# A two-layer relational graph network with two expert stages: counting spread over the edge tiles, its products three tiles later, four banks for sums, clearing in halves

## The chip, the core and the metric

The kernel runs on one core of one Trainium2 chip. The metric is the device time of one execution in microseconds (us), the median over runs. TensorE multiplies matrices, VectorE and ScalarE work on tiles, GpSimd issues the indirect row gathers, and SyncE's queue (SP) issues the other DMAs. Each engine works through its own list in order; semaphores tie the lists together.

## What is computed

The input is 2500 nodes of 256 features and 40000 edges sorted by destination, each with one of 8 relation types. Four residual blocks follow one another: a relational graph network of two layers, a mixture of experts, a three-layer graph convolution, a second mixture. The change lies in the first block, and a little of it in the third:

```python
def _rgcn_layer(x, W, self_w, b, src, dst, edge_type, num_nodes):
    xW = jnp.einsum('ni,rio->rno', x, W)
    msg = xW[edge_type, src]
    agg = jax.ops.segment_sum(msg, dst, num_segments=num_nodes)
    return agg + x @ self_w + b
...
x = x + _L0_gnn_ref(_layernorm(x, axis=-1), L0_gnn_W1, L0_gnn_self_w1, L0_gnn_b1, L0_gnn_W2, L0_gnn_self_w2, L0_gnn_b2, edge_index, edge_type_8)
x = x + _L0_ffn_ref(_layernorm(x, axis=-1)[None], L0_ffn_Wg, L0_ffn_bg, L0_ffn_W1, L0_ffn_b1, L0_ffn_W2, L0_ffn_b2)[0]
x = x + _L1_gnn_ref(_layernorm(x, axis=-1), edge_index, L1_gnn_W1, L1_gnn_b1, L1_gnn_W2, L1_gnn_b2, L1_gnn_W3, L1_gnn_b3, L1_gnn_Wp, L1_gnn_bp)
x = x + _L1_ffn_ref(_layernorm(x, axis=-1)[None], L1_ffn_Wr, L1_ffn_br, L1_ffn_ln_g, L1_ffn_ln_b, L1_ffn_W1, L1_ffn_b1, L1_ffn_W2, L1_ffn_b2)[0]
```

## The kernel before

A relational layer (`relational_layer`) walks over 313 edge tiles of 128 edges, one per step `t`. Every engine runs through the same steps in its own list, and the code of a step says what that engine issues there.

- GpSimd gathers the 128 source rows of a tile (line 1120). ScalarE makes a one-hot matrix of each edge's relation and place among 16 destinations (lines 1208 and 1211).
- TensorE multiplies rows by one-hots (`aggregate`, line 1374; each of its two products is two instructions) into one of the three PSUM banks `psS`. It may write a bank again when VectorE has added its last content: tile `t` waits for the addition of tile `t - 3`.
- VectorE adds the bank to `sums` at a place that depends on the data (`add`, lines 1267 to 1278). The place is read into a register by `value_load`, a register load in VectorE's own list, ahead of the addition.
- When a tile of 128 nodes is complete (`closed(b)`, every 16 steps), VectorE carries its rim over (`merge`) and TensorE multiplies its sums by the weights, 18 products of two instructions each (`multiply`, line 1402), spread over the steps up to `left_at(b)`. VectorE then takes the result (`take_out`, or `row_variance` and a step later `row_norm`), and SP clears the buffer with zeros by one DMA (`clear`, line 1142). There are three such buffers.

Between these lies work for later blocks:

- Counting. The third block needs how often each source occurs for each of 80 buckets of 32 destinations; layer 0 does 44 buckets, layer 1 36, one per 7 steps (`SPACING`). For a bucket VectorE makes one matrix for the sources (line 1328) and six for the pairs (`count_hots`, line 1319), in the bucket's steps 0, 2 and 4: the first of these steps has the source matrix and two pair matrices, the others two pair matrices each. Each of the three steps begins with a `value_load` of the bucket's first edge tile (line 1357). TensorE multiplies two pair matrices (line 1420) one step after each.
- Splitting of expert weights into two halves: a piece of 256 KB is loaded, ScalarE makes the high half, VectorE the low one (line 1335), SP stores both. Each layer has 48 pieces, one per 6 steps; the other 32 are split in the third block's layers (`node_layer`).

In the trace, lines 1278 (the addition), 1319, 1328 (counting) and 1374, 1402, 1420 (TensorE) are the marks to follow.

Of the kernel before, what the change touches and what calls it, by code (L numbers as in the profile page):

```python
# [71 lines left out]
LAYER_UNITS = ([*range(24, 32), *range(0, 4)], [*range(4, 8), *range(16, 24)])  # L72
# [14 lines left out]
ZEROS = SUMW // 9  # L87
STRIPS_FIRST = 11
SPACING = 7
PIECESTEP = 6  # L90
# [19 lines left out]

def left_at(b):

    return closed(b + 1) + 2 if b + 1 < TILES else closed(b) + 6
# [26 lines left out]
class Program:  # L140
# [891 lines left out]
    def relational_layer(self, layer):  # L1032
# [19 lines left out]
        psS, psO, psM, psC = [self.ps[b] for b in (0, 1, 7)], [self.ps[b] for b in (2, 6)], self.ps[3], self.ps[4:6]  # L1052
# [3 lines left out]
        steps = left_at(TILES - 1) + 7  # L1056
# [6 lines left out]
        def products_at(t):  # L1063

            b = next((b for b in range(TILES) if closed(b) + 2 <= t < left_at(b)), None)
            if b is None:
                return None, range(0)
            width, k = left_at(b) - closed(b) - 2, t - closed(b) - 2
            return b, range(PRODUCTS * k // width, PRODUCTS * (k + 1) // width)
# [10 lines left out]
        def strip_at(t):  # L1080

            i = counted_at(t, SPACING + 1)
            return buckets[i] // PER if i is not None and buckets[i] % PER == PER - 1 else None

        def piece_at(t, after):

            n, late = divmod(t - after, PIECESTEP)
            return n if late == 0 and 0 <= n < pieces else None
# [4 lines left out]
        def misc_at(t):  # L1093

            then = [("self", tile_at(closed, t))]
            if not first:
                then += [("turned", tile_at(left_at, t - 3)), ("gate", tile_at(left_at, t - 4))]
            return [(what, b) for what, b in (*then, ("degree", strip_at(t))) if b is not None]
# [4 lines left out]
        with self.stage_block() as (block, sem):  # L1103
            hot_ready, squared, summed, added, merged, out_full, out_taken, h_done, h_stored = sem(
                "hot_ready", "squared", "summed", "added", "merged", "out_full", "out_taken", "h_done", "h_stored")
            misc_full, misc_out, places_ready, src_hot, pair_hot, count_full, bank_out = sem(
# [17 lines left out]
            def _(sp):  # L1124
# [13 lines left out]
                def clear(b):  # L1138
                    sp.wait_ge(out_full, b + 1)
                    to = self.sums[:, b % SUMS * SUMW:(b % SUMS + 1) * SUMW].rearrange("p (a c) -> p a c", c=ZEROS)  # L1140
                    of = self.zero.rearrange("p (a c) -> p a c", a=1).broadcast_to([P, SUMW // ZEROS, ZEROS])
                    sp.dma_start(to, of).then_inc(cleared[b % SUMS], 16)
# [24 lines left out]
                for t in range(steps):  # L1167
                    n = piece_at(t, PIECESTEP // 2 + 2)
                    if n is not None:
                        store_piece(n)  # L1170
                    n = piece_at(t, PIECESTEP + 2)
                    if n is not None and n + 2 < pieces:
                        load_piece(n + 2)
                    b = tile_at(left_at, t)
                    if b is not None:
                        clear(b)
                        if first:
                            store_h(b)
                    b = tile_at(left_at, t - 1)
                    if b is not None and not first:  # L1180
                        store_rows(b)
                    b = strip_at(t)
                    if b is not None:
                        store_strip(b)
# [3 lines left out]
                for s in range(SUMS):  # L1188
                    sp.wait_ge(cleared[s], 16 * len(range(s, TILES, SUMS)))
# [10 lines left out]
            def _(act):  # L1200
# [45 lines left out]
                for t in range(steps):  # L1246
                    if t % GROUP == 0 and t // GROUP + HOTROWS - 1 < BATCHES:
                        onehots(t // GROUP + HOTROWS - 1)
                    b = tile_at(left_at, t)
                    if b is not None:  # L1250
                        relu(b) if first else row_root(b)
                    i = counted_at(t, SPACING - 1)
                    if i is not None:
                        take_counts(i)
                    for what, b in misc_at(t):
                        take(what, b)
                    n = piece_at(t, PIECESTEP // 2)
                    if n is not None:
                        high_piece(n)

            @block.vector
            def _(dve):
# [3 lines left out]
                def add(t):  # L1266
                    at = dve.value_load(self.at[0:1, t:t + 1], min_val=0, max_val=(SUMS - 1) * SUMW + P - 1)
                    to = self.sums[:, bass.ds(at, SUMW)].rearrange("p (s w) -> p s w", w=KEYROW)[:, :, 0:WIN]
                    dve.wait_ge(summed, t + 1)
                    if t:  # L1270
                        dve.wait_ge(added, t)
                    b = tile_at(closed, t - 1)
                    if b is not None and b + 1 < TILES:
                        dve.wait_ge(merged, b + 1)
                    b = tile_at(opened, t)
                    if b is not None and b >= SUMS:
                        dve.wait_ge(cleared[b % SUMS], 16 * (b // SUMS))
                    v.tensor_tensor(to, to, psS[t % len(psS)][:, 0:KD * P].rearrange("p (s w) -> p s w", w=WIN), ALU.add).then_inc(added, 1)  # L1278
# [6 lines left out]
                def take_out(b):  # L1285
                    dve.wait_ge(out_full, b + 1)
                    if b >= 2:
                        dve.wait_ge(h_done, b - 1)
                    v.tensor_tensor(self.hn[b % 2][:, :], psO[b % 2][:, 0:D], self.bias[:, :], ALU.add).then_inc(out_taken, 1)

                def row_variance(b):
                    x, mv = self.x_tile(b), self.mv[:, 2 * b:2 * b + 2]
                    dve.wait_ge(out_full, b + 1)
                    if b == 0:
                        dve.wait_ge(kept, 16)
                    v.tensor_tensor(x, x, psO[b % 2][:, 0:D], ALU.add).then_inc(out_taken, 1)
# [25 lines left out]
                def count_hots_from(i, at, j):  # L1322
                    k = buckets[i]
                    if j == 0:
                        if i >= 2:
                            dve.wait_ge(count_full, (i - 1) * WINDOW)
                        low = self.src_low[:, bass.ds(at, WINDOW)].rearrange("p (s c) -> p s c", c=1).broadcast_to([P, WINDOW, P])
                        v.tensor_tensor(src_hots[i % 2].rearrange("p (s c) -> p s c", s=WINDOW), places_low, low, ALU.is_equal).then_inc(src_hot, 1)
                    for n in range(j, j + 2):
                        count_hots(i, at, n)  # L1330
# [11 lines left out]
                for t in range(steps):  # L1342
# [8 lines left out]
                    b = tile_at(left_at, t - 1)  # L1351
                    if b is not None and not first:
                        row_norm(b)
                    for j in range(0, WINDOW, 2):
                        i = counted_at(t, j)
                        if i is not None:
                            at = dve.value_load(self.window[0:1, buckets[i]:buckets[i] + 1], min_val=0, max_val=ETILES - WINDOW)
                            count_hots_from(i, at, j)
                    n = piece_at(t, PIECESTEP // 2 + 1)
# [4 lines left out]
            def _(pe):  # L1364
# [22 lines left out]
                def multiply(b, which):  # L1387
                    to = psO[b % 2][:, 0:D]
                    for n in which:
                        r, k = divmod(n, KD)  # L1390
                        if n == 0:
# [4 lines left out]
                            if b >= 2:  # L1396
                                pe.wait_ge(out_taken, b - 1)
                        if n == KD * REL:
                            pe.wait_ge(misc_out, nth["self", b] + 1)
                        lhs = sum_of(b, 0, P)[:, k * REL + r, :] if r < REL else self.self_turned[b % 2][:, k * P:(k + 1) * P]  # L1400
                        at = (k * REL + r) * D if r < REL else (KD * REL + k) * D
                        last = t_.matmul(to, lhs, weights[:, at:at + D], start=(n == 0), stop=(n == PRODUCTS - 1))  # L1402
                        if n == PRODUCTS - 1:
                            last.then_inc(out_full, 1)
# [27 lines left out]
                for t in range(steps):  # L1432
# [17 lines left out]
                    for j in range(0, WINDOW, 2):  # L1450
                        i = counted_at(t, j + 1)
# [198 lines left out]
    def node_layer(self, layer):  # L1650
# [15 lines left out]
        with self.stage_block() as (block, sem):  # L1666
# [6 lines left out]
            pieces = max(0, min(TILES, UNITS // 2 * 4 - first_piece))  # L1673
# [680 lines left out]
```

## Time and profile before

| What | Value |
|---|---|
| Time, median of 3 runs | 2360.2 us (2356.88 to 2361.87) |
| The profiled execution | 2363.23 us, its span 2361.5 us |
| Additions of layer 0 (line 1278), first to last | 51.5 to 569.8 us |
| Additions of layer 1, first to last | 596.6 to 1133.7 us |
| Busy share of the span | PE 81%, PEld 69%, DVE 58%, ACT 37%, POOL 38% |

The profile names the engines PE (TensorE), PEld (its weight loads), DVE (VectorE), ACT (ScalarE), POOL (GpSimd). A name with a q, as DVEq, is the engine's own list of instructions that it doesn't count as busy: register loads, semaphore waits. The two relational layers take up almost half of the span, from about 43 to 1150 us.

### The profile page before, as it was taken

What the parts mean: (1) busy time and instruction counts of PE and PEld (TensorE: products, weight loads), DVE (VectorE), ACT (ScalarE), POOL (GpSimd) and SP (SyncE); (2) the same over time, 40 slices, a digit from 0 to 9 for tenths busy, and PEclk for the clock granted to TensorE, in tenths of its full rate; (3) what the DMA queues carried; (4) which work ended last, traced back from release to release, by engine and by line L of the source; (5) the groups of instructions that cost most, each with busy time, mean ns of one, the idle gap of its engine ahead of it and who ended that gap; (6) DMA issues with size and microseconds to landing.
All of it is one profiled execution on the core that took longest, in us unless ns stands there. A gap on an engine that the chain in (4) does not pass through costs nothing. (4 is left out here: it accounts for less than half of the span.)

```text
span 2361.5 us, 41254 instructions
## 1 busy us (share of the span) xinstructions
PE 1917.5 (81%) x11984; PEld 1625.5 (69%) x11984; DVE 1368.9 (58%) x3174; ACT 869.5 (37%) x2015; POOL 893.5 (38%) x859
## 2 busy tenths in 40 slices
PE   3778888887677787788479999949989875899987
PEld 2566666666566666667369999837878765799977
DVE  4666666563566666665455555564645566566654
ACT  4434444341543333443013333334544431333332
POOL 3776565550776555554013433330000000333332
PEclk8999999999898899998769999979999975999998
DMA  6676677663676666666564633245766457324261
GB/s 215 211 238 220 217 222 226 216 219 119 218 240 209 198 209 202 201 220 200 176 263 109 203 64 100 32 142 199 252 206 214 136 205 284 119 42 119 41 201 23
DMA packets 204784, 420.87 MB, mean 178 GB/s; under 512 B 24837, under 2 KB 115953, under 8 KB 200433
## 3 DMA queue, kind: packets, MB, share of 16 engines
q1 hardware_dynamic: 153864, 308.52, 37.3%
q0 software_dynamic: 48096, 106.74, 18.4%
q10 hardware_dynamic: 2568, 2.56, 0.3%
q8 instruction: 117, 1.92, 0.3%
q14 instruction: 139, 1.13, 0.2%
HBM read 256.77 MB, written 113.77 MB: 157 GB/s over the span
## 5 line engine op out<-in xcount | busy, mean ns | idle before, releaser
L2193 PE MATMUL ps<-ring,halves 128*128 x3384 | 581.7, 327 | 17.0 <-SPq L2155 9.3
L2193 PEld LDWEIGHTS ps<-ring,halves 128*128 128x128 f32 x3384 | 485.9, 192 | 61.7 <-issue 18.8
L1278 DVE TENSOR_TENSOR sums<-sums,ps 128x256 f32 x626 | 263.3, 421 | 304.0 <-PE ps L1374 223.2
L1374 PEld LDWEIGHTS ps<-slots,rows 128*128 128x128 f32 x2504 | 393.6, 207 | 61.4 <-ACT slots L1211 26.8
L1374 PE MATMUL ps<-slots,rows 128*128 128x128 f32 x2504 | 406.3, 290 | 25.9 <-DMA rows<-tab_h,gidx_node 14.2
L1120 POOL DMA_INDIRECT rows<-tab_h,gidx_node x313 | 312.6, 999 | 260.0 <-PE ps L1374 117.1
L1402 PE MATMUL ps<-fixed,sums 128*128 128x256 f32 x1280 | 390.8, 400 | 0.2 <-DVE sums L1283 0.2
L1120 POOL DMA_INDIRECT rows<-tab_x,gidx_node x313 | 311.5, 995 | 203.9 <-PE ps L1374 91.8
L1420 PE MATMUL ps<-scratch,fixed 128*128 128x320 f16 x960 | 198.9, 322 | 195.0 <-DVE scratch L1319 189.9
L1420 PEld LDWEIGHTS ps<-scratch,fixed 128*128 128x128 f16 x960 | 65.6, 100 | 329.4 <-DVE scratch L1319 169.9
L2302 ACT ACTIVATE x_all<-ps 128x512 f32<-128x512 f32 x188 | 113.2, 602 | 467.8 <-PE ps L2212 467.8
L1208 ACT ACTIVATE slots<-iota,dst_in_bucket 128x128 f32<-128x128 f32 x626 | 199.2, 390 | 223.0 <-PE ps L1374 213.1
L1859 PE MATMUL ps<-node_rows,blocks 128*128 128x512 f32 (+1 forms) x1200 | 258.7, 367 | 0.1
L1319 DVE TENSOR_SCALAR scratch<-fixed,scratch,count_key 128x640 f16<-128x640 f16 x480 | 198.9, 456 | 72.0 <-issue 71.8
L1859 PEld LDWEIGHTS ps<-node_rows,blocks 128*128 128x128 f32 x1200 | 203.8, 195 | 30.9 <-ACT blocks L1741 0.6
L2260 DVE TENSOR_TENSOR halves<-x_all,halves 128x512 fp32r<-128x512 f32 x188 | 130.2, 692 | 147.5 <-ACT halves L2303 147.5
L1402 PEld LDWEIGHTS ps<-fixed,sums 128*128 128x128 f32 x1280 | 211.6, 201 | 5.2 <-DVE sums L1283 0.6
L1959 POOL IOTA x_all<- 128x20 f32 x2 | 0.3, 148 | 437.7 <-POOLq L214 437.7
L2170 POOL DMA_INDIRECT out<-x_all,place_of_slot x47 | 74.6, 1588 | 205.4 <-ACT x_all L2310 170.7
L2170 POOL DMA_INDIRECT x_sum<-x_all,place_of_slot x47 | 74.4, 1582 | 192.4 <-ACT x_all L2310 149.4
L2270 DVE TENSOR_TENSOR whole<-ps,acc 128x512 f32<-128x512 f32 x188 | 121.2, 686 | 39.7 <-PE ps L2193 35.1
L2162 POOL DMA_INDIRECT x_all<-tab_node,token_of_slot x94 | 93.6, 996 | 122.7 <-POOLq L214 82.3
(245 smaller groups left out, 2144.0 us busy)
## 6 DMA issues: line engine op xcount, KB each, us to landing
ring<-split_weights SPq DMA_DIRECT2D x16, 4096.0 KB, 15.1
split_weights<-fixed SPq DMA_DIRECT2D x192, 256.0 KB
sums<-fixed SPq DMA_DIRECT2D x40, 1152.0 KB, 6.8
slots<-tab_counts SPq DMA_DIRECT2D x40, 640.0 KB, 4.1
fixed<-in_ffn_units SPq DMA_DIRECT2D x96, 256.0 KB, 3.7
split_weights<-weight_pieces SPq DMA_DIRECT2D x64, 256.0 KB, 2.5
tab_counts<-fixed SPq DMA_DIRECT2D x20, 640.0 KB, 5.4
strip<-tab_counts SPq DMA_DIRECT2D x20, 640.0 KB, 4.1
```

What stands on the lines that cost most here:

```text
L1120: nc.gpsimd.indirect_dma_start(rows[:, s * D:(s + 1) * D], None, table, bass.IndirectOffsetOnAxis(ap=gidx[:, t:t + 1], axis=0)).then_inc(g ...
L1208: last = nc.scalar.activation(to[:, j * P:(j + 1) * P], self.iota[:, 0:P], ACT.Square, scale=-1.0, bias=self.rel[:, t:t + 1])
L1278: v.tensor_tensor(to, to, psS[t % len(psS)][:, 0:KD * P].rearrange("p (s w) -> p s w", w=WIN), ALU.add).then_inc(added, 1)
L1319: v.tensor_scalar(pair_hots[j], places, base[:, buckets[i]:buckets[i] + 1], self.key[:, bass.ds(at + j, 1)], ALU.add, ALU.is_equal).then_i ...
L1374: last = t_.matmul(psS[t % len(psS)][:, k * P:(k + 1) * P], rows[:, s * D + k * P:s * D + (k + 1) * P], self.onehots[:, h * P:(h + 1) * P] ...
L1402: last = t_.matmul(to, lhs, weights[:, at:at + D], start=(n == 0), stop=(n == PRODUCTS - 1))
L1420: last = t_.matmul(psC[h][:, 0:half], src_hots[i % 2][:, n * P:(n + 1) * P], pair_hots[n][:, h * half:(h + 1) * half], start=(n == 0), sto ...
L1859: last = nc.tensor.matmul(to, self.blocks[b % 2][:, g * P:(g + 1) * P], self.node_tile(layer, g), start=False, stop=(g == TILES - 1))
L2170: nc.gpsimd.indirect_dma_start(to, bass.IndirectOffsetOnAxis(ap=self.place[:, i:i + 1], axis=0), yout[i % 2], None, compute_op=ALU.add).th ...
L2193: ins = nc.tensor.matmul(to, lhs[left], weights(slot, right, at, n), start=first and (left, right) == (0, 0), stop=last and left == 1)
L2260: nc.vector.tensor_tensor(hT_low[:, b * 512:(b + 1) * 512], hT[:, b * 512:(b + 1) * 512], hT_high[:, b * 512:(b + 1) * 512], ALU.subtract) ...
L2270: last = nc.vector.tensor_tensor(h[:, b * 512:(b + 1) * 512], psH[b][:, :], bias(e, b * 512, 512), ALU.add)
```

## The change

Everything stands in `relational_layer`, apart from constants and one line of `node_layer`.

- Counting: each of a bucket's 7 steps gets one piece: step 0 the source matrix, steps 1 to 6 one pair matrix each. Every one of them is behind a `value_load` of its own. TensorE's products of a bucket come at its steps 5, 7 and 9 (`COUNTED`), each three steps behind the second pair matrix that it reads; ScalarE takes the counts at step 10 (`TAKEN`).
- Banks: `psS` has four banks, so `aggregate` waits for the addition of tile `t - 4`. `psO`, the result of `multiply`, has one bank and waits until VectorE has taken the tile before.
- `multiply` begins three steps after `closed(b)` (`begun`) and is spread over 12 steps, first the products of the buffer's first half, then those of the second. SP clears each half by a DMA of its own, in rows of 384 elements where there were 256.
- ScalarE's and VectorE's row work behind `take_out` and `row_variance` comes one to three steps later than before.
- Weight pieces: one per 7 steps, 44 in each layer; 40 where there were 32 in `node_layer`.

```diff
@@ -69,7 +69,8 @@
-LAYER_UNITS = ([*range(24, 32), *range(0, 4)], [*range(4, 8), *range(16, 24)])
+NODEUNITS = 10
+LAYER_UNITS = ([*range(24, 32), *range(0, 3)], [*range(3, 8), *range(18, 24)])
...
-ZEROS = SUMW // 9
+ZEROS = SUMW // KD // 3
...
-PIECESTEP = 6
+COUNTED = 5
+TAKEN = 10
+HIGHPIECE = 1
+LOWPIECE = 4
...
+def begun(b):
+
+    return closed(b) + 3 if b + 1 < TILES else left_at(b - 1)
+
+
 def left_at(b):
 
-    return closed(b + 1) + 2 if b + 1 < TILES else closed(b) + 6
+    return closed(b) + 15 if b + 1 < TILES else begun(b) + 4
...
-        psS, psO, psM, psC = [self.ps[b] for b in (0, 1, 7)], [self.ps[b] for b in (2, 6)], self.ps[3], self.ps[4:6]
+        psS, psO, psM, psC = [self.ps[b] for b in (0, 1, 6, 7)], self.ps[2], self.ps[3], self.ps[4:6]
...
-                def clear(b):
-                    sp.wait_ge(out_full, b + 1)
...
+                def clear(b, k):
+                    sp.wait_ge(half_used, KD * b + k + 1)
...
+                    b = tile_at(begun, t - 6)
+                    if b is not None:
+                        clear(b, 0)
+                    b = tile_at(left_at, t)
+                    if b is not None:
+                        clear(b, 1)
...
-                def count_hots_from(i, at, j):
-                    k = buckets[i]
-                    if j == 0:
-                        if i >= 2:
-                            dve.wait_ge(count_full, (i - 1) * WINDOW)
...
-                    for n in range(j, j + 2):
-                        count_hots(i, at, n)
...
-                    for j in range(0, WINDOW, 2):
-                        i = counted_at(t, j)
-                        if i is not None:
-                            at = dve.value_load(self.window[0:1, buckets[i]:buckets[i] + 1], min_val=0, max_val=ETILES - WINDOW)
-                            count_hots_from(i, at, j)
-                    n = piece_at(t, PIECESTEP // 2 + 1)
+                    i, late = divmod(t, SPACING)
+                    if i < len(buckets):
+                        at = dve.value_load(self.window[0:1, buckets[i]:buckets[i] + 1], min_val=0, max_val=ETILES - WINDOW)
+                        if late:
+                            count_hots(i, at, late - 1)
+                        else:
+                            source_hots(i, at)
+                    n = piece_at(t, LOWPIECE)
...
-                        r, k = divmod(n, KD)
+                        k, r = divmod(n, REL)
...
-                        i = counted_at(t, j + 1)
+                        i = counted_at(t, j + COUNTED)
...
-            pieces = max(0, min(TILES, UNITS // 2 * 4 - first_piece))
+            pieces = max(0, min(TILES, NODEUNITS * 4 - first_piece))
```

On VectorE in layer 0 this is a bucket's first counting step before, with the next step's addition behind it. `TENSOR_LOAD window` is the counting's register load, `TENSOR_LOAD fixed` that of the addition; an `ISA` row is register arithmetic or a wait.

```order
L1357 TENSOR_LOAD window
L1357 ISA x2
L1328 ISA [waits set0_14]
L1328 TENSOR_TENSOR fixed<-iota,src_in_tile 128x768
L1319 ISA [waits set0_14]
L1319 TENSOR_SCALAR scratch<-fixed,scratch,count_key 128x640
L1319 ISA [waits set0_14]
L1319 TENSOR_SCALAR scratch<-fixed,scratch,count_key 128x640
L1267 TENSOR_LOAD fixed
L1267 ISA x2
L1278 ISA [waits set0_3,set0_2]
L1278 TENSOR_TENSOR sums<-sums,ps 128x16x16
```

And the same place after the change (lines 1341, 1334, 1282 and 1293 are the former 1328, 1319, 1267 and 1278).

```order
L1367 TENSOR_LOAD window
L1367 ISA x2
L1341 ISA [waits set0_15]
L1341 TENSOR_TENSOR fixed<-iota,src_in_tile 128x768
L1282 TENSOR_LOAD fixed
L1282 ISA x2
L1293 ISA [waits set0_3,set0_2]
L1293 TENSOR_TENSOR sums<-sums,ps 128x16x16
L1367 TENSOR_LOAD window
L1367 ISA x2
L1334 ISA [waits set0_15]
L1334 TENSOR_SCALAR scratch<-fixed,scratch,count_key 128x640
```

The two pair matrices have left the step; from here on additions and single pieces of counting alternate, with a register load ahead of each. Over both layers the list has 560 loads of `window` where it had 240, and 626 of `fixed` as before.

On TensorE in layer 0, steps of tiles with the same gathered rows before: the counting products (line 1420) wait for the pair matrices (`set0_13`) made in VectorE's step just before.

```order
L1374 MATMUL ps<-slots,rows 128x128 [waits gathered18,set0_3,set0_0]
L1374 MATMUL ps<-slots,rows 128x128
L1402 MATMUL ps<-fixed,sums 128x256
L1420 MATMUL ps<-scratch,fixed 128x320 [waits set0_13,set0_15,set0_12]
L1420 MATMUL ps<-scratch,fixed 128x320
L1420 MATMUL ps<-scratch,fixed 128x320 [waits set0_13]
L1420 MATMUL ps<-scratch,fixed 128x320
L1374 MATMUL ps<-slots,rows 128x128 [waits gathered19,set0_3,set0_0]
```

After (1387, 1416 and 1436 are the former 1374, 1402 and 1420):

```order
L1387 MATMUL ps<-slots,rows 128x128 [waits gathered22,set0_3,set0_0]
L1387 MATMUL ps<-slots,rows 128x128
L1416 MATMUL ps<-fixed,sums 128x256 [waits set0_6,set0_4]
L1436 MATMUL ps<-scratch,fixed 128x320 [waits set0_14,set0_16,set0_13]
L1436 MATMUL ps<-scratch,fixed 128x320
L1436 MATMUL ps<-scratch,fixed 128x320 [waits set0_14]
L1436 MATMUL ps<-scratch,fixed 128x320
L1387 MATMUL ps<-slots,rows 128x128 [waits gathered23,set0_3,set0_0]
```

A bucket's first products have moved four tiles on, and the products of a node tile begin one tile later than they did.

## Rows read from the trace of the kernel before

**Rows 1.** The page's busy time of each engine: us, share of span, instructions.
```profile
PE 1917.5 (81%) x11984; PEld 1625.5 (69%) x11984; DVE 1368.9 (58%) x3174; ACT 869.5 (37%) x2015; POOL 893.5 (38%) x859
```

**Rows 2.** Windows: layer 0's additions; layer 1 while it counts, and after.
```profile
core 0: us, PE busy (x) PEld busy (x) DVE busy (x) ACT busy (x) POOL busy (x), PEclk, DMA share, GB/s
51.40:569.90 518.50, 417.64 (x2705) 323.61 (x2706) 317.62 (x706) 209.32 (x551) 304.84 (x307) 0.94 0.67 213
596.50:1053.85 457.35, 355.25 (x2234) 279.29 (x2235) 291.66 (x716) 183.25 (x498) 274.72 (x275) 0.90 0.66 209
1053.85:1134.20 80.35, 70.32 (x441) 64.72 (x440) 41.44 (x115) 26.20 (x72) 31.41 (x33) 0.92 0.61 197
```

**Rows 3.** Waits, whole span: who for whom, us in total, times, longest.
```profile
DVE sums L1278 <- PE ps L1374: 223.2, 301, 8.7
...
PE ps L1420 <- DVE scratch L1319: 189.9, 151, 5.5
```

**Rows 4.** VectorE's own list, lines 1267 and 1357: ns minimum/median/maximum, first and last.
```profile
L1267 DVEq TENSOR_LOAD <-fixed x626: 297/308/1483, 42.9 to 1132.9; - x157
L1267 DVEq FUSED_REGOPS  x626: 190/190/206, 43.5 to 1133.3; - x157
...
L1357 DVEq TENSOR_LOAD <-window x240: 297/304/1176, 51.5 to 1050.2; - x120
```

**Rows 5.** Timeline of VectorE, two quiet places: start, length, what, idle before.
```profile
73.32 0.42 DVE L1278 TENSOR_TENSOR sums<-sums,ps 128x256 f32 x1 [0.41 <-PE ps L1374]
74.14 0.42 DVE L1278 TENSOR_TENSOR sums<-sums,ps 128x256 f32 x1 [0.40 <-PE ps L1374]
74.89 0.96 DVE L1328 TENSOR_TENSOR fixed<-iota,src_in_tile 128x768 f16<-128x768 f32 x1 [0.33 <-issue]
75.77 0.80 DVE L1319 TENSOR_SCALAR scratch<-fixed,scratch,count_key 128x640 f16<-128x640 f16 x2
76.48 0.41 DVE L1278 TENSOR_TENSOR sums<-sums,ps 128x256 f32 x1
...
317.30 0.42 DVE L1278 TENSOR_TENSOR sums<-sums,ps 128x256 f32 x1 [0.53 <-PE ps L1374]
318.07 0.80 DVE L1319 TENSOR_SCALAR scratch<-fixed,scratch,count_key 128x640 f16<-128x640 f16 x2 [0.35 <-issue]
319.04 0.42 DVE L1278 TENSOR_TENSOR sums<-sums,ps 128x256 f32 x1 [0.17 <-issue]
```

**Rows 6.** Timeline of VectorE while a buffer is being cleared.
```profile
306.16 0.96 DVE L1319 TENSOR_SCALAR scratch<-fixed,scratch,count_key 128x640 f16<-128x640 f16 x2 [0.71 <-issue]
307.82 0.42 DVE L1278 TENSOR_TENSOR sums<-sums,ps 128x256 f32 x1 [0.69 <-issue]
309.67 0.42 DVE L1278 TENSOR_TENSOR sums<-sums,ps 128x256 f32 x1 [1.44 <-PE ps L1374]
```

**Rows 7.** Line 1267's register loads, from 302 to 311 us.
```profile
L1267 DVEq TENSOR_LOAD <-fixed x5: 394/681/1332, 302.9 to 309.7; - x5
```

**Rows 8.** Line 1267's register loads, from 312 to 320.5 us.
```profile
L1267 DVEq TENSOR_LOAD <-fixed x7: 297/305/416, 312.2 to 320.0; - x7
```

**Rows 9.** DMA issues of both layers: count, KB each, median us to landing.
```profile
sums<-fixed SPq DMA_DIRECT2D x39, 1152.0 KB, 6.8
```

**Rows 10.** Timeline of TensorE around a wait.
```profile
308.34 0.61 PE L1374 MATMUL ps<-slots,rows 128*128 128x128 f32 x4
308.79 0.60 PE L1402 MATMUL ps<-fixed,sums 128*128 128x256 f32 x2
309.22 0.61 PE L1374 MATMUL ps<-slots,rows 128*128 128x128 f32 x4
...
313.27 0.71 PE L1420 MATMUL ps<-scratch,fixed 128*128 128x320 f16 x4 [3.01 <-DVE scratch L1319]
313.82 0.61 PE L1374 MATMUL ps<-slots,rows 128*128 128x128 f32 x4
```

**Rows 11.** Windows: the third block's layers, which split the other pieces.
```profile
1600.00:1918.00 318.00, 301.05 (x1650) 257.95 (x1650) 173.47 (x383) 150.77 (x250) 0.00 (x0) 0.96 0.59 198
```

More of the change, by code:

```diff
@@ L1055, in relational_layer @@
             g.base += 16 * len(range(s, ETILES, RINGROWS))
-        steps = left_at(TILES - 1) + 7
+        steps = left_at(TILES - 1) + 10
         def sum_of(b, at, n):
@@ L1063, in products_at @@
         def products_at(t):
-            b = next((b for b in range(TILES) if closed(b) + 2 <= t < left_at(b)), None)
+            b = next((b for b in range(TILES) if begun(b) <= t < left_at(b)), None)
             if b is None:
                 return None, range(0)
-            width, k = left_at(b) - closed(b) - 2, t - closed(b) - 2
+            width, k = left_at(b) - begun(b), t - begun(b)
             return b, range(PRODUCTS * k // width, PRODUCTS * (k + 1) // width)
@@ L1080, in strip_at @@
         def strip_at(t):
-            i = counted_at(t, SPACING + 1)
+            i = counted_at(t, TAKEN + 2)
             return buckets[i] // PER if i is not None and buckets[i] % PER == PER - 1 else None
         def piece_at(t, after):
-            n, late = divmod(t - after, PIECESTEP)
+            n, late = divmod(t - SPACING - after, SPACING)
             return n if late == 0 and 0 <= n < pieces else None
@@ L1096, in misc_at @@
             if not first:
-                then += [("turned", tile_at(left_at, t - 3)), ("gate", tile_at(left_at, t - 4))]
+                then += [("turned", tile_at(left_at, t - 6)), ("gate", tile_at(left_at, t - 9))]
             return [(what, b) for what, b in (*then, ("degree", strip_at(t))) if b is not None]
@@ L1105, in relational_layer @@
                 "hot_ready", "squared", "summed", "added", "merged", "out_full", "out_taken", "h_done", "h_stored")
+            half_used = sem("half_used")
             misc_full, misc_out, places_ready, src_hot, pair_hot, count_full, bank_out = sem(
@@ L1136, in store_piece @@
                     sp.dma_start(to[:, 1, :], piece_raw[n % 2]).then_inc(piece_stored[n % 2], 16)
-                def clear(b):
-                    sp.wait_ge(out_full, b + 1)
-                    to = self.sums[:, b % SUMS * SUMW:(b % SUMS + 1) * SUMW].rearrange("p (a c) -> p a c", c=ZEROS)
-                    of = self.zero.rearrange("p (a c) -> p a c", a=1).broadcast_to([P, SUMW // ZEROS, ZEROS])
+                def clear(b, k):
+                    sp.wait_ge(half_used, KD * b + k + 1)
+                    at = b % SUMS * SUMW + k * SUMW // KD
+                    to = self.sums[:, at:at + SUMW // KD].rearrange("p (a c) -> p a c", c=ZEROS)
+                    of = self.zero.rearrange("p (a c) -> p a c", a=1).broadcast_to([P, SUMW // KD // ZEROS, ZEROS])
                     sp.dma_start(to, of).then_inc(cleared[b % SUMS], 16)
@@ L1167, in _ @@
                 for t in range(steps):
-                    n = piece_at(t, PIECESTEP // 2 + 2)
+                    b = tile_at(begun, t - 6)
[4 more added lines that the diff above has]
+                        clear(b, 1)
+                    b = tile_at(left_at, t - 2)
+                    if b is not None and first:
+                        store_h(b)
+                    b = tile_at(left_at, t - 4)
+                    if b is not None and not first:
+                        store_rows(b)
+                    n = piece_at(t, LOWPIECE + 1)
                     if n is not None:
                         store_piece(n)
-                    n = piece_at(t, PIECESTEP + 2)
+                    n = piece_at(t, LOWPIECE + 4)
                     if n is not None and n + 2 < pieces:
                         load_piece(n + 2)
[L1174 to L1181, printed above, removed]
                     b = strip_at(t)
@@ L1188, in _ @@
                 for s in range(SUMS):
-                    sp.wait_ge(cleared[s], 16 * len(range(s, TILES, SUMS)))
+                    sp.wait_ge(cleared[s], 16 * KD * len(range(s, TILES, SUMS)))
                 if first:
@@ L1248, in _ @@
                         onehots(t // GROUP + HOTROWS - 1)
-                    b = tile_at(left_at, t)
+                    b = tile_at(left_at, t - 1)
                     if b is not None:
                         relu(b) if first else row_root(b)
-                    i = counted_at(t, SPACING - 1)
+                    i = counted_at(t, TAKEN)
                     if i is not None:
@@ L1256, in _ @@
                         take(what, b)
-                    n = piece_at(t, PIECESTEP // 2)
+                    n = piece_at(t, HIGHPIECE)
                     if n is not None:
@@ L1276, in add @@
                     if b is not None and b >= SUMS:
-                        dve.wait_ge(cleared[b % SUMS], 16 * (b // SUMS))
+                        dve.wait_ge(cleared[b % SUMS], 16 * KD * (b // SUMS))
                     v.tensor_tensor(to, to, psS[t % len(psS)][:, 0:KD * P].rearrange("p (s w) -> p s w", w=WIN), ALU.add).then_inc(added, 1)
@@ L1288, in take_out @@
                         dve.wait_ge(h_done, b - 1)
-                    v.tensor_tensor(self.hn[b % 2][:, :], psO[b % 2][:, 0:D], self.bias[:, :], ALU.add).then_inc(out_taken, 1)
+                    v.tensor_tensor(self.hn[b % 2][:, :], psO[:, 0:D], self.bias[:, :], ALU.add).then_inc(out_taken, 1)
                 def row_variance(b):
@@ L1295, in row_variance @@
                         dve.wait_ge(kept, 16)
-                    v.tensor_tensor(x, x, psO[b % 2][:, 0:D], ALU.add).then_inc(out_taken, 1)
+                    v.tensor_tensor(x, x, psO[:, 0:D], ALU.add).then_inc(out_taken, 1)
                     dve.wait_ge(out_taken, b + 1)
@@ L1320, in count_hots, with source_hots @@
                                     ALU.add, ALU.is_equal).then_inc(pair_hot, 1)
-                def count_hots_from(i, at, j):
-                    k = buckets[i]
-                    if j == 0:
-                        if i >= 2:
-                            dve.wait_ge(count_full, (i - 1) * WINDOW)
-                        low = self.src_low[:, bass.ds(at, WINDOW)].rearrange("p (s c) -> p s c", c=1).broadcast_to([P, WINDOW, P])
-                        v.tensor_tensor(src_hots[i % 2].rearrange("p (s c) -> p s c", s=WINDOW), places_low, low, ALU.is_equal).then_inc(src_hot, 1)
-                    for n in range(j, j + 2):
-                        count_hots(i, at, n)
+                def source_hots(i, at):
+                    if i >= 2:
+                        dve.wait_ge(count_full, (i - 1) * WINDOW)
+                    low = self.src_low[:, bass.ds(at, WINDOW)].rearrange("p (s c) -> p s c", c=1).broadcast_to([P, WINDOW, P])
+                    v.tensor_tensor(src_hots[i % 2].rearrange("p (s c) -> p s c", s=WINDOW), places_low, low, ALU.is_equal).then_inc(src_hot, 1)
                 def low_piece(n):
@@ L1350, in _ @@
                         take_out(b) if first else row_variance(b)
-                    b = tile_at(left_at, t - 1)
+                    b = tile_at(left_at, t - 3)
                     if b is not None and not first:
                         row_norm(b)
-                    for j in range(0, WINDOW, 2):
-                        i = counted_at(t, j)
-                        if i is not None:
-                            at = dve.value_load(self.window[0:1, buckets[i]:buckets[i] + 1], min_val=0, max_val=ETILES - WINDOW)
-                            count_hots_from(i, at, j)
-                    n = piece_at(t, PIECESTEP // 2 + 1)
+                    i, late = divmod(t, SPACING)
[6 more added lines that the diff above has]
+                    n = piece_at(t, LOWPIECE)
                     if n is not None:
@@ L1387, in multiply @@
                 def multiply(b, which):
-                    to = psO[b % 2][:, 0:D]
+                    to = psO[:, 0:D]
                     for n in which:
-                        r, k = divmod(n, KD)
+                        k, r = divmod(n, REL)
                         if n == 0:
@@ L1395, in multiply @@
                                 pe.wait_ge(added, ETILES)
-                            if b >= 2:
-                                pe.wait_ge(out_taken, b - 1)
-                        if n == KD * REL:
+                            if b:
+                                pe.wait_ge(out_taken, b)
+                        if k < KD:
+                            lhs, at = sum_of(b, 0, P)[:, n, :], (k * REL + r) * D
+                        else:
                             pe.wait_ge(misc_out, nth["self", b] + 1)
-                        lhs = sum_of(b, 0, P)[:, k * REL + r, :] if r < REL else self.self_turned[b % 2][:, k * P:(k + 1) * P]
-                        at = (k * REL + r) * D if r < REL else (KD * REL + k) * D
+                            lhs, at = self.self_turned[b % 2][:, r * P:(r + 1) * P], (KD * REL + r) * D
                         last = t_.matmul(to, lhs, weights[:, at:at + D], start=(n == 0), stop=(n == PRODUCTS - 1))
+                        if k < KD and r == REL - 1:
+                            last.then_inc(half_used, 1)
                         if n == PRODUCTS - 1:
```

## The prediction

> **What bounds the kernel now.** The page's busy shares come first [rows 1]: TensorE is busy for 81% of the span and VectorE for 58%, so VectorE looks like the engine with room. The windows say the same of the two layers [rows 2]: while layer 0 adds, TensorE is busy for 418 of 518 us and VectorE for 318. The waits then show two engines waiting for each other [rows 3]: TensorE idles 190 us ahead of counting products (line 1420) until VectorE's pair matrices are there, and VectorE idles 223 us ahead of additions (line 1278) that are put down to TensorE.
>
> The second of these is misleading, and VectorE's own list shows why. Every addition is behind a register load of its place, every counting step behind one of its bucket [rows 4]. A load takes 0.30 us at least, the register arithmetic behind it 0.19, and the timeline shows what the whole chain is worth where nothing else is late [rows 5]: two additions follow each other by 0.82 us (73.32 to 74.14), although one takes 0.42; the row names TensorE for the 0.40 between. From an addition to a pair matrix are 0.77 us (317.30 to 318.07), to a source matrix 0.75. So what limits VectorE is its list: it can't load ahead of the instruction in front, and hides a load behind one VectorE operation at most. At 75.77 two pair matrices were queued behind a long source matrix, and there the next addition came 0.71 us later, with its load hidden; behind a lone pair of matrices it came after 0.97 (318.07 to 319.04).
>
> The second thing in the list is that a load is often long: at most 1.48 us [rows 4]. While a buffer is cleared, five loads have a median of 0.68 us [rows 7]; just after it, seven have 0.305 [rows 8]. In the first stretch a counting step with its addition takes 1.66 us from pair matrix to addition (306.16 to 307.82), and addition to addition 1.85 (307.82 to 309.67) [rows 6], twice the quiet values. TensorE's wait of 3.01 us at 313.27 [rows 10] is what these slow additions left behind. So VectorE's list paces the two layers, not its busy time.
>
> **The change part by part.** *Register loads.* A bucket has 7 counting loads where it had 3. I compare 7 quiet steps. Now: four plain additions at 0.82, two pair steps at 0.77 + 0.97, one source step at 0.75 + 0.88 + 0.71 [rows 5]; that is 3.28 + 3.48 + 2.34 = 9.10 us. After: six steps of one addition and one pair matrix, and one with the source matrix. Addition to matrix stays 0.77. From a lone matrix to the next addition no row of before shows. Below it is bounded by the matrix alone, 0.40 (half of 0.80), if the load were hidden; above by an operation with a load behind it, 0.82. I take 0.82, since the chain is the same and 0.40 is too short to cover it. Behind the source matrix (0.96 long) I take its 0.88 to the next operation. So 6 x (0.77 + 0.82) + 0.75 + 0.88 = 11.17 us, or 2.07 more per bucket: 91 us for layer 0's 44 buckets, 75 for layer 1's 36, **+166**.
>
> *Long loads.* A clear lands in 6.8 us [rows 9], once in 16 steps, which take 16 x 518.5 / 312 = 26.6 us [rows 2]: a quarter of the time loads cost 0.38 us more (0.681 against 0.305) [rows 7, 8], 0.10 on average. The piece transfers are on the same queue; with them I estimate 0.13 per load, so 113 us now for 866 loads [rows 4]. After, 1186 loads would pay 154, 41 more, if each is as likely to be hit; since the bytes that SP moves are the same and the layers get longer, about half of that if the time under transfer decides. I take **+30**. The halves are written in longer rows, but they are the same bytes.
>
> *Waits that go.* TensorE's products now follow their matrices by three steps, and the fourth bank lets TensorE run a tile further ahead; both waits of [rows 3] lose their cause. For VectorE this is worth only what of the 223 us was really waiting: 301 times 0.40 is the chain itself (74.14 in [rows 5]), 120 us; long loads at 0.13 are another 39; 64 remain. I take **-55**, bounded by 0 and -103 (no long load among them). TensorE's own 190 us give nothing more: they only turn into waits for additions.
>
> *The rest* I cost at nothing. Merging, taking out and row work keep their operations and are in both sums. Clearing takes 80 DMAs for 40 on SP, ahead of SP's stores; a half is asked for 10 steps (16 us) before its buffer is opened again, and lands within 6.8 [rows 9]; without that cover an addition, all of VectorE's list behind it, and four tiles later TensorE would wait. The single result bank makes TensorE wait for the result's taking, which stands four steps ahead in VectorE's list, and TensorE is not what paces. Eight pieces move to the third block's layers, where TensorE is busy for 301 of 318 us and VectorE for 173 [rows 11]: hidden; uncovered they would cost 8 x 0.69, under 6 us.
>
> The sum: 166 + 30 - 55 = +141 on the profiled execution's 2363.2 us, 2504. That execution lies 3 us above the median of the runs, so I forecast **2501** us for the median. By the bounds: with no long load left (-113) and the 64 us of waits gone it is 166 - 177 = -11, 2349; with 41 more and no wait gone +207, 2567.
>
> **The rivals.** *TensorE becomes the bound, and the kernel is much faster.* If VectorE could load ahead, its work per step would be 0.42 + 0.40 us, and TensorE would pace: 0.45 for a tile's aggregation (308.34 to 308.79), 36 weight products per 16 steps at 0.215 (0.43 for two), 0.48, and 12 counting products per 7 steps at 0.55 for four, 0.24 [rows 10]; 1.17, at the granted clocks of 0.94 and 0.90 [rows 2] 1.24 and 1.30. Layer 0 would need 388 us instead of 518, the counting part of layer 1 328 instead of 457: 259 less, 2101. For it speak the waits [rows 3] and VectorE's busy share; against it that idle of 0.33 to 0.40 us stands before every loaded operation, with no other cause [rows 5]. It decides where a step costs less than the present 1.66 us of layer 0; by my quiet rows it is 1.60 before any long load or tile work. The Trainium skill, page "Perfetto Trace Analysis", is on this rival's side: occupancy is for VectorE a fair measure of how near its limit it is ("Identifying the Most-Contended Engine"), and where VectorE isn't saturated but causes bubbles on other engines, breaking up instructions may let work complete sooner ("Optimizing Scalar/DVE Operations"). By that rule the sum would be this rival's, not mine; the trace disagrees in that VectorE's list is full at a busy share of 61%.
>
> *Long loads become rare.* Halves at other times, in longer rows, may disturb less. If half of the 113 us goes, the sum is 166 - 57 - 55 = +54, 2414; if all, no change or 2349. Against it: the bytes are the same.
>
> *New waits take the place of the old.* If the waits of VectorE don't go, because results, clears or matrices are late in the new order, and each load pays in full: 2567 and more.
>
> **How the numbers follow.** My forecast (2440 to 2565) 0.78; long loads rarer 0.10, of which 0.03 is within 0.2% of now; TensorE the bound, or partly so, 0.06; new waits 0.06. 0.2% is about what a measurement of this kernel can tell from no change. Range 2435 to 2575, which leaves out the fast rival and most of the second. Faster 0.07, same 0.03, slower 0.90.
>
> **What would show it.** `TENSOR_LOAD <-window` x560; in a quiet place 0.77 us from addition to pair matrix and 0.82 from there to the next addition; the additions of layer 0 from first to last in about 596 us, the first 252 steps of layer 1 in about 520; no TensorE wait for pair matrices, waits for additions in its place, and a lower busy share of TensorE. I am wrong if a lone pair matrix is followed by its addition in much less than 0.82, if loads under a clear are short, or if the additions come 1.3 us apart.

## The result, and the profile after

The changed kernel takes 2471.8 us (2470.25 to 2488.29, 4 runs) where the kernel before takes 2359.7: a ratio of 1.0492, with a 95% interval of 1.0446 to 1.0537. It is 112 us slower; 141 were forecast. The profiled execution has a span of 2468.5 us, 107 more than before.

The windows of the same stretches as in [rows 2] (same columns, here with the new times of the first and last additions) show where: layer 0's additions 54 us longer, layer 1's counting part 53, layer 1's rest 4 shorter.

```profile
51.20:623.90 572.70, 448.29 (x2694) 350.82 (x2694) 328.45 (x701) 207.01 (x548) 306.30 (x306) 0.90 0.58 185
652.40:1162.30 509.90, 379.80 (x2259) 299.34 (x2260) 298.28 (x709) 179.52 (x495) 276.92 (x279) 0.87 0.56 179
1162.30:1238.30 76.00, 64.38 (x404) 57.70 (x403) 42.04 (x117) 25.83 (x73) 27.84 (x29) 0.91 0.65 217
```

By its share of the first stretch no engine is busier: VectorE's falls from 61 to 57%, TensorE's from 81 to 78%. The granted clock, a mean over the stretch, is lower too, 0.90 for 0.94, and TensorE's busy time for the same products rose from 418 to 448 us. It is not the new places that lower the clock: in e1 below, with the same products in the same places, it is 0.97 and the busy time 386. How much of the 112 us the lower clock carries was not separated. The waits of [rows 3] are still there in part (line 1387 is the former 1374, 1436 the former 1420), and the last one listed is new:

```profile
DVE scratch L1334 <- issue: 173.7, 397, 1.5
...
PE ps L1436 <- DVE scratch L1334: 144.5, 158, 3.9
DVE sums L1293 <- PE ps L1387: 127.8, 185, 8.9
...
DVE sums L1293 <- issue: 121.2, 270, 1.6
...
PE ps L1416 <- DVE sums L1298: 54.3, 32, 3.8
```

The idle time that grew is "issue" ahead of pair matrices and additions (174 and 121 us), in which the engine waits for nothing that the profile shows. In the kernel before it was 72 and 62:

```profile
DVE scratch L1319 <- issue: 71.8, 159, 1.4
...
DVE sums L1278 <- issue: 62.4, 139, 1.6
```

What happens there is in VectorE's own list: 560 loads of `window` against 240 in [rows 4].

```profile
L1282 DVEq TENSOR_LOAD <-fixed x626: 296/306/1550, 42.4 to 1237.2; - x157
L1367 DVEq TENSOR_LOAD <-window x560: 296/302/1410, 51.3 to 1159.9; - x187
```

And this is a quiet place on VectorE's timeline, to be held against [rows 5]:

```profile
300.67 0.42 DVE L1293 TENSOR_TENSOR sums<-sums,ps 128x256 f32 x1 [0.38 <-issue]
301.44 0.45 DVE L1334 TENSOR_SCALAR scratch<-fixed,scratch,count_key 128x640 f16<-128x640 f16 x1 [0.35 <-issue]
302.26 0.42 DVE L1293 TENSOR_TENSOR sums<-sums,ps 128x256 f32 x1 [0.37 <-issue]
303.04 0.45 DVE L1334 TENSOR_SCALAR scratch<-fixed,scratch,count_key 128x640 f16<-128x640 f16 x1 [0.35 <-issue]
```

From addition to matrix 0.77 and 0.78 us, from a lone matrix to the next addition 0.82: 1.59 us per step, for 0.87 us of work.

### The profile page after: what moved, and what is told of

Same layout as the page of the kernel before. It is cut to its first block and busy times, and to the rows that moved or that the text cites. A ratio compares the mean times of both kernels' runs of the same rounds, so it can differ in the third digit from the quotient of the medians.

```text
span 2468.5 us, 42256 instructions
## 1 busy us (share of the span) xinstructions
PE 1972.6 (80%) x11984; PEld 1670.6 (68%) x11984; DVE 1393.6 (56%) x3174; ACT 867.1 (35%) x2015; POOL 893.5 (36%) x859
## 5 line engine op out<-in xcount | busy, mean ns | idle before, releaser
L1387 PE MATMUL ps<-slots,rows 128*128 128x128 f32 x2504 | 427.5, 300 | 71.2 <-issue 35.3
L1416 PE MATMUL ps<-fixed,sums 128*128 128x256 f32 x1280 | 388.8, 419 | 55.6 <-DVE sums L1298 54.3
L1334 DVE TENSOR_SCALAR scratch<-fixed,scratch,count_key 128x640 f16<-128x640 f16 x480 | 219.5, 457 | 205.2 <-issue 173.7
L1436 PE MATMUL ps<-scratch,fixed 128*128 128x320 f16 x960 | 217.7, 326 | 147.3 <-DVE scratch L1334 144.5
L1416 PEld LDWEIGHTS ps<-fixed,sums 128*128 128x128 f32 x1280 | 234.2, 210 | 79.6 <-DVE sums L1298 61.8
L1436 PEld LDWEIGHTS ps<-scratch,fixed 128*128 128x128 f16 x960 | 81.8, 103 | 252.2 <-DVE scratch L1334 199.1
```

The lines of the kernel that those rows point to most:

```text
L1334: v.tensor_scalar(pair_hots[j], places, base[:, buckets[i]:buckets[i] + 1], self.key[:, bass.ds(at + j, 1)], ALU.add, ALU.is_equal).then_i ...
L1387: last = t_.matmul(psS[t % len(psS)][:, k * P:(k + 1) * P], rows[:, s * D + k * P:s * D + (k + 1) * P], self.onehots[:, h * P:(h + 1) * P] ...
L1436: last = t_.matmul(psC[h][:, 0:half], src_hots[i % 2][:, n * P:(n + 1) * P], pair_hots[n][:, h * half:(h + 1) * half], start=(n == 0), sto ...
```

## The experiments

Each is compared with the kernel before as timed beside it (2361.8 us for e1 to e4, 2359.5 for e5 to e8).

**e1, one register load per bucket in the changed kernel.**

```diff
                     if i < len(buckets):
-                        at = dve.value_load(self.window[0:1, buckets[i]:buckets[i] + 1], min_val=0, max_val=ETILES - WINDOW)
+                        if not late:
+                            at = dve.value_load(self.window[0:1, buckets[i]:buckets[i] + 1], min_val=0, max_val=ETILES - WINDOW)
```

> The changed kernel with one register load of the bucket's first tile per bucket (at its step 0, kept in the register for the other six pieces) instead of seven; 80 loads of window for 560. Nothing else differs. Theory (VectorE's list of register loads paces the layers): a step with a pair matrix becomes about 1.0 us from addition to addition for 1.59, 7.6 us per quiet bucket for 11.2; TensorE at 1.24 to 1.30 us per step then paces much of it. Expected 2200 us (2150 to 2260). Rival (the new places of products, clears, the single result bank or the moved pieces cost the time, and the loads only fill waits): it stays at 2440 or more.

2193.9 us, a ratio of 0.9299 (0.9270 to 0.9328) to the kernel before: 278 us off the changed kernel, with no other line touched. On its timeline a matrix is right behind its addition, and the step of two operations has shrunk to 0.90 and 0.98 us (303.97, 304.87, then 306.19 to 307.17; between them, at 306.19, VectorE did wait for TensorE):

```profile
303.97 0.42 DVE L1293 TENSOR_TENSOR sums<-sums,ps 128x256 f32 x1
304.30 0.44 DVE L1334 TENSOR_SCALAR scratch<-fixed,scratch,count_key 128x640 f16<-128x640 f16 x1
304.87 0.42 DVE L1293 TENSOR_TENSOR sums<-sums,ps 128x256 f32 x1
305.21 0.44 DVE L1334 TENSOR_SCALAR scratch<-fixed,scratch,count_key 128x640 f16<-128x640 f16 x1
306.19 0.42 DVE L1293 TENSOR_TENSOR sums<-sums,ps 128x256 f32 x1 [0.55 <-PE ps L1388]
306.53 0.44 DVE L1334 TENSOR_SCALAR scratch<-fixed,scratch,count_key 128x640 f16<-128x640 f16 x1
307.17 0.42 DVE L1293 TENSOR_TENSOR sums<-sums,ps 128x256 f32 x1 [0.20 <-issue]
```

TensorE now is busy for 386 of layer 0's 425 us; that it paces most of it is borne out by e7. The rival, by which the new places cost the time, falls.

**e2, counting back in three steps, the rest of the change kept.**

```diff
-                    i, late = divmod(t, SPACING)
...
+                    for j in range(0, WINDOW, 2):
+                        i = counted_at(t, j)
+                        if i is not None:
+                            at = dve.value_load(self.window[0:1, buckets[i]:buckets[i] + 1], min_val=0, max_val=ETILES - WINDOW)
+                            if j == 0:
+                                source_hots(i, at)
+                            for n in range(j, j + 2):
+                                count_hots(i, at, n)
```

> The changed kernel with the counting matrices back in three steps (source and two, two, two; three register loads per bucket), everything else of the change kept: products three steps behind, four banks, halves cleared, one result bank, 44 pieces. Theory: the loads are those of before (quiet bucket 9.10 us), the waits between the engines are gone: 2305 us (2280 to 2345). Rival (the rest of the change costs the time): 2440 or more.

2289.2 us, 0.9702 (0.9668 to 0.9736). The rest of the change is worth 73 us, and TensorE's wait for pair matrices is gone from its list of waits. So the spreading alone costs 2471.8 - 2289.2 = 183 us. It brings two things: 320 loads, and a shorter lead, for in e2 both matrices of a product are made five steps ahead of it and in the changed kernel four and three. With the loads gone (e4 and e1) the second costs nothing.

**e3, one register load per bucket in the kernel before.**

```diff
-                            at = dve.value_load(self.window[0:1, buckets[i]:buckets[i] + 1], min_val=0, max_val=ETILES - WINDOW)
+                            if j == 0:
+                                at = dve.value_load(self.window[0:1, buckets[i]:buckets[i] + 1], min_val=0, max_val=ETILES - WINDOW)
```

> The kernel before with one register load per bucket for three; nothing else differs. Theory: 160 loads fewer, a pair step goes from 1.74 to 1.33 us, 0.8 per bucket, 66 us, and 160 loads' share of the long ones, about 15, less where VectorE then waits for TensorE: 2295 us (2260 to 2335). Rival (VectorE has time to spare, its loads are covered by waits for TensorE): 2355 to 2365.

2287.7 us, 0.9685 (0.9649 to 0.9721). 160 loads fewer give 74 us in the old order too: VectorE's list paced the kernel before as well, as the prediction read it.

**e4, e2 and one load per bucket.** The edits of e2, with the load under `if j == 0`.

> As e2 (three counting steps, rest of the change), with one register load per bucket. Theory: the gains of e2 and e3 add up, since both are on VectorE's list: 2240 us (2200 to 2290), and above e1, whose quiet bucket is 7.6 us against 8.3 here. Rival (the rest of the change costs the time): 2400 or more.

2205.5 us, 0.9336 (0.9300 to 0.9372). Alone, 160 fewer loads gave 74 us (e3) and the rest of the change 73 (e2), 147 together; both at once give 156, so the gains add up, and a little more. It was expected at 2240; a load was worth more than I put it at. Beside e1 it shows what spreading is worth once its loads are gone: 11 us, or 0.5%, which is hardly clear of noise (e1's runs reach 2200.3, those of e4 begin at 2197.1).

**e5, four more loads per bucket in the kernel before.**

```diff
+                    i, late = divmod(t, SPACING)
+                    if i < len(buckets) and late not in (0, 2, 4):
+                        dve.value_load(self.window[0:1, buckets[i]:buckets[i] + 1], min_val=0, max_val=ETILES - WINDOW)
```

> The kernel before with four more register loads per bucket, in the four steps of a bucket that count nothing; their values aren't used, and nothing else differs. 560 loads of window as in the changed kernel. Theory (the number of loads sets the time): a plain step goes from 0.82 to 1.59 us, 3.1 us per quiet bucket, 246 for 80 buckets, less up to 55 of waits for TensorE that they cover: 2575 us (2530 to 2620). Rival (loads fill waits for TensorE): under 2400.

2521.5 us, 1.0693 (1.0648 to 1.0738), a little under the range given. Loads without any use make the old order slower than the change, by 50 us. A quiet plain step takes 1.45 us rather than the 1.59 expected. A value that no operation uses lacks the register arithmetic on the operation's own line, 0.064 us in the median at line 1334 of the changed kernel; that is part of the 0.14, the rest is open:

```profile
74.15 0.42 DVE L1278 TENSOR_TENSOR sums<-sums,ps 128x256 f32 x1 [0.37 <-issue]
75.60 0.42 DVE L1278 TENSOR_TENSOR sums<-sums,ps 128x256 f32 x1 [1.03 <-PE ps L1377]
77.03 0.42 DVE L1278 TENSOR_TENSOR sums<-sums,ps 128x256 f32 x1 [1.01 <-issue]
```

The second row has its idle put down to TensorE, the third to nothing; the interval is the same, and the load is the cause of both. So 0.63 us for each of 320 loads, 202 us, of which 162 are seen in the time.

**e6, the changed kernel without its clears.**

```diff
-                    sp.dma_start(to, of).then_inc(cleared[b % SUMS], 16)
+                    sp.dma_start(to[:, 0:1, 0:1], of[:, 0:1, 0:1]).then_inc(cleared[b % SUMS], 16)
```

> The changed kernel with every clearing DMA cut to one element per partition, so that the buffers keep old sums and the output is not the reference's; waits and order are the same. It tells what makes register loads long. Theory (loads are long while SP's transfers run, the clears above all): long loads become rare, and up to two thirds of their cost in the changed kernel (about 113 us over both layers) goes: 2400 us (2370 to 2440), the longest load still over 1 us because of the pieces. Rival (long loads come from GpSimd's gathers or from VectorE's own writes): no change, 2460 to 2485.

2398.6 us, 1.0165 (1.0126 to 1.0204) to the kernel before, 73 us under the changed kernel. Of the 66 us between the two profiled spans, 56 lie between the first and last additions of the two layers (1158 us, here 1102). The longest load of a place is 1.19 us for 1.55:

```profile
L1282 DVEq TENSOR_LOAD <-fixed x626: 296/304/1185, 43.1 to 1181.3; - x157
```

Summed from the records of the loads in each trace, what they take over their quiet 0.302 us:

```
kernel   loads of window   loads of places   us over 0.302 each
before        240               625               110
changed       560               625               114
e1             80               625               117
e2            240               625               104
e4             80               625               101
e5            560               625               113
e6            560               625                58
e7             80               157                54
```

About half goes with the clears, 56 us, as much as the layers' additions are shorter by; that agreement suggests, but does not show, that it is through the loads that a clear costs time. With the clears in place the sum hardly depends on how many loads there are, from 705 to 1185. With the 237 of e7, each load of a place there reading four values, it is half as large, so the number does count when it falls that far.

**e7, e1 with the places of four additions in one register load.**

```diff
-                    at = dve.value_load(self.at[0:1, t:t + 1], min_val=0, max_val=(SUMS - 1) * SUMW + P - 1)
+                    if t % GROUP == 0:
+                        n = min(GROUP, ETILES - t)
+                        _, values = nc.values_load_multi_w_load_instructions(
+                            self.at[0:1, t:t + n], engines=(mybir.EngineType.DVE,), min_val=0, max_val=(SUMS - 1) * SUMW + P - 1)
+                        for k in range(n):
+                            ats[t + k] = values[k]
+                    at = ats.pop(t)
```

> e1 with the places of four additions read by one register load (157 loads for 626). Theory (VectorE's list still paces part of e1): VectorE's step falls to about 0.9 us and TensorE paces nearly alone, at 1.25 to 1.35 us per step: 2125 us (2090 to 2165). Rival (e1 is already bound by TensorE): within 15 us of e1's 2194.

2166.1 us, 0.9185 (0.9149 to 0.9222): the fastest of all, and 28 us under e1, where 69 were expected and the rival gave up to 15; it lies just outside the range given. The theory overrates it: TensorE paces most of e1 already. It is busy for 380 of layer 0's 409 us here, 93%, and waits for additions for 4.1 us in all of that stretch:

```profile
51.60:460.60 409.00, 380.31 (x2673) 327.00 (x2673) 292.97 (x701) 205.91 (x546) 310.71 (x306) 0.98 0.79 258
```

**e8, e2 with three banks for the sums.**

```diff
-        psS, psO, psM, psC = [self.ps[b] for b in (0, 1, 6, 7)], self.ps[2], self.ps[3], self.ps[4:6]
+        psS, psO, psM, psC = [self.ps[b] for b in (0, 1, 7)], self.ps[2], self.ps[3], self.ps[4:6]
```

> e2 (counting in three steps, rest of the change kept) with three banks for the sums instead of four. Theory: with the products three steps behind, TensorE rarely needs the fourth bank, since VectorE's list paces: 2290 to 2310, within 20 us of e2's 2289. Rival (the fourth bank is what e2 gains by): 2340 to 2360.

2289.2 us, 0.9699 (0.9661 to 0.9737), the same as e2. In that order the fourth bank gives nothing. Which of the other parts brings the 73 us, the later products or the earlier clears, was not separated.

## Why the prediction was right, step by step

**What paces the layers: right, and shown.** Five pairs of kernels differ in the register loads of `window` (and in the second pair in the places too), and the time per load is 0.46 to 0.58 us, about the 0.52 of the prediction's 166 us for 320:

```
pair                       loads   us    us per load
before -> e3                -160   -74      0.46
e2 -> changed               +320  +183      0.57
changed -> e1               -480  -278      0.58
e2 -> e4                    -160   -84      0.52
before -> e5                +320  +162      0.51
```

The quiet prices were right to the hundredth: 0.77 and 0.82 us, where the second was chosen from bounds of 0.40 and 0.82. Over both layers of the changed kernel the medians are the same, 0.77 from an addition to the pair matrix right behind it (411 intervals) and 0.82 from a matrix to the addition right behind it (402). The +166 for a quiet bucket is not measured apart from the long loads; together they were put at 196, and the spreading alone (e2 to the changed kernel) took 183. The layers themselves came out shorter than I wrote: layer 0's additions took 573 us and not 596, the first 252 steps of layer 1 took 510 and not 520.

**Long loads: mis-sized.** Their term was +30. The table under e6 has 110 us before and 114 after, +4; counted from e2, where the spreading starts, 104 and 114, +10. The step that failed is the estimate "about half of that if the time under transfer decides": 320 more loads met hardly more delay in sum. Nor were SP's bytes quite "the same": a layer splits 44 pieces for 48. That their source is SP's traffic was only argued, from [rows 7, 8]; e6 shows it for half of the sum. The rest, pieces or other traffic, was not tried.

**Waits that go: the size held, the reason only half.** The term was -55; e2 measures the whole rest of the change, waits included, at -73. But [rows 3] did not "lose their cause": in the changed kernel TensorE still waits 144.5 us for pair matrices, where I expected waits at the additions instead. It is VectorE's pace that leaves them: in e1, with the same places and 480 loads fewer, they come to 10.6 us (line 1437 is 1436 there):

```profile
PE ps L1437 <- DVE scratch L1334: 10.6, 13, 2.0
```

In e2, with fewer loads and a longer lead, they are gone. The fourth bank, which I named for this, has no part in it (e8).

Counted by way of e2, with +10 for +30 and -73 for -55, the sum is 166 + 10 - 73 = +103 against the 112 measured. The 9 us between are not accounted for; 2 of them lie in the kernel before, timed at 2361.8 beside e2 and at 2359.7 beside the change. The two errors, 20 and 18 us, point the same way and the 9 against them: that the forecast was no more than 29 us too high is in part luck, while the mechanism, loads on VectorE's list, is shown.

**At no cost.** The third block's layers, with eight more pieces, took as long as before: their products began at 1707.2 us and the last one at 2025.5, 318.3 us apart; 318.1 before. Clears and the single result bank left no new wait to be seen in VectorE's list. TensorE has one that it did not have: 54.3 us ahead of weight products for VectorE's merged sums (line 1298), 0.2 before. In e1, much the faster kernel, that wait is still 46.5 us, so it is not what makes the change slow.

**The rivals.** "TensorE becomes the bound" failed for the reason given, that VectorE can't load ahead. Its price was three quarters right for another kernel: with most loads gone (e7) TensorE does pace, and the gain is 193 of the 259 us promised. The rule from the Trainium skill, page "Perfetto Trace Analysis", is that breaking up instructions of an unsaturated engine that causes bubbles on others may let work complete sooner ("Optimizing Scalar/DVE Operations"). Here whole instructions were spread and none was broken up, so this is a neighbour of that rule; the spreading lost 183 us with loads of its own, and without them gained some 11, from 2205.5 in e4 to 2193.9 in e1, hardly more than noise. "Long loads become rare" is out by the e6 table; "new waits" by e2.

## What to carry to other kernels

An engine's busy share leaves out its own instruction list. Where an operation is addressed by a register, count the loads in that list and take the interval from one operation to the next, not its duration; a wait put down to another engine at just that interval can be the load's, as in e5. When work is spread over more places, ask what each place brings along: here one value kept in a register, and four read at once, turned a loss of 5% into a gain of 8%, of which 3% is the rest of the change (e2).

## What was not expected of the hardware

What the loads take over their quiet time came to 101 to 117 us over the two layers for anything from 705 to 1185 loads, and to 54 for 237. And one register load of four values takes hardly longer than one of a single value, 0.344 us in the median against 0.308; the register arithmetic of 0.19 us stays, once for each of the 626 values:

```profile
L1286 DVEq TENSOR_LOAD <-fixed x158: 318/344/1385, 42.7 to 926.0; - x158
```
